# Feed-forward layer one moved to the transposes' banks, a tanh gate, expert scores from rows before their last normalisation, and self attention 8 groups behind cross attention

## The reference

```
x = LN(x + attention_1head(x))                        # W1..W4, 112x112 scores
t = crossattn(x, context, 16 heads of 16, mask);  t = LN(t @ co + x) * g + b
t = selfattn(t, 16 heads of 16);                  t = LN(t @ so + t) * g + b
t = LN(gelu(t @ fi + fib) @ fo + t) * g + b           # 256 -> 1024 -> 256
x = LN(x + t)                                         # "x5"
scores = x @ centroids.T; expert = argmax; alpha = sigmoid(score of the chosen)
y = x + relu(LN(x)*gamma_e+beta_e @ W1_e + b1_e) @ W2_e + b2_e     # 8 experts
x = LN(alpha*y + (1-alpha)*x)
```

## Time and profile before

| what | value |
|---|---|
| median of 3 runs | 472.16 us |
| profiled execution, its own time | 475.34 us |
| its span | 473.3 us |
| TensorE busy | 414.8 us (88%) |
| VectorE, ScalarE, GpSimd busy | 270.6, 243.3, 127.8 us |
| granted TensorE clock, mean | 0.939 |

### The profile page before, as it was taken

How to read it: one execution, slowest core, us unless ns; L and a number is a source line. 1 busy time by engine, 2 the same in 40 slices (tenths; PEclk the granted TensorE clock), 3 DMA queues, 4 the chain that set the end, 5 groups by cost and what they waited for, 6 DMA issues and landing times.

```text
span 473.3 us, 10486 instructions
## 1 busy us (share of the span) xinstructions
PE 414.8 (88%) x3672; PEld 347.0 (73%) x3672; DVE 270.6 (57%) x936; ACT 243.3 (51%) x822; POOL 127.8 (27%) x256
## 2 busy tenths in 40 slices
PE   6888999999999999999979797967988358998991
PEld 6766778878787887878768686756878247997991
DVE  4486766685666876867655255357255651443522
ACT  0305785785689878887887735520433002322320
POOL 4271202131032221212222132234043306231323
PEclk9999999999999999999989987985998669999997
DMA  8994100101010060000000980004802012111001
GB/s 224 304 383 100 38 10 16 35 15 35 2 48 2 2 225 2 16 1 3 1 2 2 366 345 1 1 11 176 377 10 90 29 56 81 35 34 35 25 24 35
DMA packets 10341, 37.87 MB, mean 80 GB/s; under 512 B 1440, under 2 KB 5776, under 8 KB 8400
## 3 DMA queue, kind: packets, MB, share of 16 engines
q1 hardware_dynamic: 8064, 28.40, 17.4%
q10 hardware_dynamic: 976, 5.60, 3.4%
q0 software_dynamic: 1248, 3.18, 2.1%
HBM read 32.13 MB, written 5.04 MB: 79 GB/s over the span
## 4 chain that ended last, share of the span: by engine, by line
PE 52%; DVE 6%; ACT 5%; issue 5%; DMA 2%; POOL 1%; DVEq 0%; POOLq 0%; ACTq 0%; SPq 0%
PE bank_scores L674 8%; PE bank_pt L572 7%; PE bank_out L689 7%; PE bank_scores L610 6%; PE bank_out L619 5%; PE bank_out L460 4%; PE bank_scores L556 3%; PE bank_out L446 3%; PE bank_out L594 2%; ACT arena L1080 2%; PE bank_scores L562 2%; PE bank_out L453 2%; ACT arena L1069 1%; DVE stats L747 1%; ACT arena L1089 1%
## 5 line engine op out<-in xcount | busy, mean ns | idle before, releaser
L1089 ACT ACTIVATE arena<-bank_pt 125x448 f32<-125x448 f32 (+1 forms) x128 | 67.4, 546 | 71.3 <-PE bank_pt L572 66.2
L572 PE MATMUL bank_pt<-ident,arena 112*125 112x112 f32 (+1 forms) x512 | 75.3, 280 | 4.5 <-ACT arena L1095 2.6
L870 DVE CUSTOM_DVE_ANT_0 arena<-bank_scores,arena 112x375 f32<-112x375 f32 x128 | 64.6, 544 | 25.3 <-PE bank_scores L562 18.0
L1069 ACT ACTIVATE arena<-arena,negmaxc 112x375 f32<-112x375 f32 x128 | 76.9, 604 | 2.6 <-DVE negmaxc L870 2.4
L572 PEld LDWEIGHTS bank_pt<-ident,arena 112*125 112x125 f32 (+1 forms) x512 | 63.2, 177 | 16.5 <-ACT arena L1089 6.4
L460 PE MATMUL bank_out<-arena 128*112 128x256 f32 (+1 forms) x224 | 59.3, 392 | 2.5 <-DVE arena L836 0.9
L1169 POOL TENSOR_TENSOR vareps<-meanvar,scal 112x1 f32<-112x1 f32 (+1 forms) x50 | 9.7, 194 | 173.6 <-DVE meanvar L750 128.5
L1124 ACT ACTIVATE arena<-bank_scores,consts 128x128 f32<-128x128 f32 x80 | 22.9, 370 | 60.0 <-PE bank_scores L674 46.0
L446 PE MATMUL bank_out<-arena 128*128 128x112 f32 x320 | 42.7, 288 | 5.2 <-POOL scal L1140 4.4
L460 PEld LDWEIGHTS bank_out<-arena 128*112 128x112 f32 (+1 forms) x224 | 37.9, 186 | 11.6 <-issue 3.3
L446 PEld LDWEIGHTS bank_out<-arena 128*128 128x128 f32 x320 | 41.0, 201 | 6.9 <-POOL scal L1140 4.3
(11 more groups left out here) (153 smaller groups left out, 634.2 us busy)
## 6 DMA issues: line engine op xcount, KB each, us to landing
arena<-moe SPq DMA_DIRECT2D x8, 2048.0 KB, 13.5
arena<-ctxT SPq DMA_DIRECT2D x8, 375.0 KB, 5.9
arena<-weights ACTq DMA_DIRECT2D x2, 1024.0 KB, 18.6
arena<-mask SPq DMA_DIRECT2D x8, 164.1 KB, 3.5
x_slots<-arena SPq DMA_DIRECT2D x8, 130.0 KB, 25.0
arena<-x_slots SPq DMA_DIRECT2D x8, 130.0 KB
arena<-fi ACTq DMA_DIRECT2D x1, 1024.0 KB, 24.0
arena<-fo ACTq DMA_DIRECT2D x1, 1024.0 KB, 27.2
```

The lines of the kernel that those rows point to most:

```text
L572: last = nc.tensor.transpose(dst[0:kp, j * S:(j + 1) * S], probs[0:S, (n % 2) * HG + j, c * kp:(c + 1) * kp], ident[0:S, 0:S])
L870: v.tensor_tensor_reduce(out=probsC[0:S, i % (2 * HG)], in0=score_bank[j][0:S, 0:KX], in1=masks[0:S, u % 2], scale=-1.0, scalar=3.0e38, op ...
L1069: a.activation(probsC[0:S, i % (2 * HG)], probsC[0:S, i % (2 * HG)], ACT.Exp, bias=negmax["c"][0:S, u, at:at + 1], scale=-1.0, accum_out=s ...
L1089: a.activation(probsT[0:kp, n % RT, c], pt_bank[PT[stage, i] % RP][0:kp, 0:HG * S], ACT.Copy).then_inc(pt_free, 1)
```

## The change

Five things, in one new order of the list:

- f1 writes to the two transposes' banks, in pieces that fill 448 columns of one bank: 2 chunks for two batches, 4 chunks for one, 16 pieces in all. Each piece is an entry of its own in the list, with its own due number. qk no longer waits for f1, and f2 waits piece by piece.
- The gate is 0.25 + 0.25 * tanh(best / 2). VectorE makes best * rstd * 0.5, ScalarE the Tanh, VectorE one step more.
- The transposes zx read the row before its last normalisation (behind zf, not zb). The scores with the centroids are then corrected: gap = src - mean * sum(centroid), and the largest gap is chosen; the division by the deviation enters only in the gate. The sums of the centroids come from two more matmuls in aw.
- LAG is 8, so there are 40 rounds, the last 8 with self attention alone.
- The tables of due numbers are others, with a further table SHIFT of some 240 single steps.

```diff
-ROUNDS = FC // RS
+PIECES = [FC * len(batches) * S // 448 for batches, _ in FEED]
+FIRST_PIECE = [sum(PIECES[:q]) for q in range(len(FEED) + 1)]
...
-LAG = 10
+LAG = 8
...
-FEED_STAGES = {"f1": 0.35, "f2": 1.69, "zf": 2.6, "zb": 3.72, "zn": 4.52, "zx": 4.62, "sc": 5.75, "rk": 6.77}
+FEED_STAGES = {"f1": -0.71, "f2": 0.66, "zf": 1.61, "zb": 3.44, "zn": 3.66, "zx": 3.44, "sc": 4.76, "rk": 5.85}
+PIECE_PACE = (0.14,)
+SHIFT = {("zx", 0): -0.04, ("aqk", 0): -0.01, ("aw", 0): -0.13, ("at", 0): -0.17, ("av", 0): -0.01, ("ab", 0): -0.09,
...
-PT, _ = number({"as": 1, "at": 1, "ct": 1, "st": 1, "pr": 1})
+PT, _ = number({"as": 1, "at": 1, "ct": 1, "st": 1, "pr": 1, "f1": 1})
...
-SCORED, _ = number({"qk": 1, "f1": RS})
+SCORED, _ = number({"qk": 1})
...
+                    pe.wait_ge(setup, 10)
+                    dst = out_slot(slot + C + 1)
+                    for k in range(C):
+                        last = mm(dst[0:S, 0:E], ones[:, 0:S], consts[:, COLS["cent"] + k * E:COLS["cent"] + (k + 1) * E],
+                                  start=k == 0, stop=k == C - 1)
+                    last.then_inc(out_full, 1)
...
-                    opened = {"a": "ay", "c": "cy", "s": "sy", "z": "zf"}[kind]
-                    pe.wait_ge(norm_done, FINISHED[FINISHES[opened], i] + 1)
-                    transposed_rows(slot, x1[0:S, i] if kind in "az" else ybuf[0:S, OPENED[opened, i] % NR])
+                    opened, finished = {"a": ("ay", "ab"), "c": ("cy", "cb"), "s": ("sy", "sb"), "z": ("zf", "zf")}[kind]
+                    pe.wait_ge(norm_done, FINISHED[finished, i] + 1)
+                    transposed_rows(slot, x1[0:S, i] if kind == "a" else ybuf[0:S, OPENED[opened, i] % NR])
...
-                    for b in range(RS):
-                        f = h * RS + b
-                        score_slots((stage, i), b)
+                    dst = pt_slot(PT[stage, i])
+                    for at, f in enumerate(chunks_of):
                         for k in range(C):
-                            last = mm(score_bank[b][:, 0:n], fi_sb[:, k, f * 128:(f + 1) * 128], x3T[:, k, batches[0] * S:batches[0] * S + n],
-                                      start=k == 0, stop=k == C - 1)
-                        last.then_inc(score_full, 1)
+                            last = mm(dst[:, at * n:(at + 1) * n], fi_sb[:, k, f * 128:(f + 1) * 128],
+                                      x3T[:, k, batches[0] * S:batches[0] * S + n], start=k == 0, stop=k == C - 1)
+                    last.then_inc(pt_full, 1)
...
-                    pe.wait_ge(hidden_ready, FC * (q + 1))
                     dst = out_slot(slot)
-                    for f in range(FC):
-                        last = mm(dst[0:S, 0:D], hiddenT[:, q % 2, f, j * S:(j + 1) * S], fo_sb[:, f], start=f == 0, stop=f == FC - 1)
+                    for p in range(FIRST_PIECE[q], FIRST_PIECE[q + 1]):
+                        pe.wait_ge(hidden_ready, HIDDEN["f1", p] + 1)
+                        for f in pieces(p)[3]:
+                            last = mm(dst[0:S, 0:D], hiddenT[:, q % 2, f, j * S:(j + 1) * S], fo_sb[:, f], start=f == 0, stop=f == FC - 1)
...
-                    v.tensor_reduce(best[0:S, i:i + 1], src[0:S, 0:E], AX.X, ALU.max).then_inc(best_ready, 1)
-                    dve.wait_ge(best_ready, i + 1)
-                    v.scalar_tensor_tensor(marked[0:S], src[0:S, 0:E], best[0:S, i:i + 1], rev[0:S], ALU.is_equal, ALU.mult)\
+                    dve.wait_ge(stats_ready, k + 1)
+                    v.scalar_tensor_tensor(gap[0:S], minus_centroids[0:S], meanvar[0:S, k % NR, 0:1], src[0:S, 0:E], ALU.mult, ALU.add)\
                         .then_inc(out_free, 1)
                     dve.wait_ge(out_free, slot + 1)
+                    v.tensor_reduce(best[0:S, i:i + 1], gap[0:S], AX.X, ALU.max).then_inc(best_ready, 1)
+                    dve.wait_ge(best_ready, i + 1)
+                    link(v.scalar_tensor_tensor(marked[0:S], gap[0:S], best[0:S, i:i + 1], rev[0:S], ALU.is_equal, ALU.mult))
+                    linked()
...
+                    dve.wait_ge(rstd_ready, k + 1)
+                    v.tensor_scalar(best[0:S, i:i + 1], best[0:S, i:i + 1], rstd[0:S, k % NR], 0.5, ALU.mult, ALU.mult).then_inc(best_scaled, 1)
...
-                    link(v.tensor_scalar(ex[0:S, i:i + 1], ex[0:S, i:i + 1], 1.0, 2.0, ALU.add, ALU.mult))
-                    linked()
-                    v.reciprocal(xrows[0:S, i, ALPHA:ALPHA + 1], ex[0:S, i:i + 1]).then_inc(alphaed, 1)
+                    v.tensor_scalar(xrows[0:S, i, ALPHA:ALPHA + 1], ex[0:S, i:i + 1], 0.25, 0.25, ALU.mult, ALU.add).then_inc(alphaed, 1)
...
-                    act.wait_ge(best_ready, i + 1)
-                    a.activation(ex[0:S, i:i + 1], best[0:S, i:i + 1], ACT.Exp, scale=-1.0).then_inc(exped, 1)
+                    act.wait_ge(best_scaled, i + 1)
+                    a.activation(ex[0:S, i:i + 1], best[0:S, i:i + 1], ACT.Tanh).then_inc(exped, 1)
```

More of the change, by code:

```diff
@@ L331, in pt_read, with scores_read, pieces @@
             stage = stage_of_pt[n]
+            if stage[0] == "f1":
+                return hidden_ready, HIDDEN[stage] + 1
             return (probs_ready, PROBS[stage] + 1) if stage[0] == "as" else (pt_free, COPIED[stage] + 1)
-        rounds = [stage for stage in STEPS if stage[0] in ("qk", "f1")]
-        def scores_read(stage, b):
-            kind, n = stage
-            if kind == "f1":
-                return [(hidden_ready, HIDDEN[stage] + b + 1)]
+        def scores_read(n, b):
             return [(scores_masked, n * HG + b + 1)] * (n < GROUPS) + [(probs_ready, PROBS["sm", n - LAG] + b + 1) for _ in range(n >= LAG)]
+        def pieces(i):
+            q = next(q for q in range(len(FEED)) if i < FIRST_PIECE[q + 1])
+            batches, per = FEED[q][0], FC // PIECES[q]
+            return q, batches, len(batches) * S, range((i - FIRST_PIECE[q]) * per, (i - FIRST_PIECE[q] + 1) * per)
         def all_probs(kind, n):
@@ L428, in out_slot @@
                 return out_bank[n % RO]
-            def score_slots(stage, banks):
-                k = rounds.index(stage)
-                for read in scores_read(rounds[k - 1], banks) if k else ():
-                    pe.wait_ge(*read)
             def pt_slot(n):
@@ L548, in _ @@
                 elif stage == "qk":
-                    score_slots((stage, i), HG - 1)
+                    for read in scores_read(i - 1, HG - 1) if i else ():
+                        pe.wait_ge(*read)
                     if i < GROUPS:
@@ L598, in _ @@
                 elif stage == "f1":
[L599 to L601 removed]
+                    q, batches, n, chunks_of = pieces(i)
+                    if i == FIRST_PIECE[q]:
                         if q == 0:
```

73 lines of the change are left out of this document (37 added, 36 removed), and 39 rows, old and new, of the table SHIFT.

## The result

The changed kernel takes 444.32 us (median of 4 runs, 442.99 to 445.75), before 472.67 us (4 runs on the same chip, 472.06 to 473.27). The ratio is 0.9413, 95% interval 0.9391 to 0.9435: 5.9% faster. Of the named cases rival B (the clock stays full, 448.8) is the nearest.

What follows compares the result with a forecast made beforehand. TensorE bounds it: dense in cross attention, then 18.7 us idle at clock 0.88 from 220 to 360 us. Terms -8.5 - 7.0 - 0.9 + 1.0 + 0.5 = -14.9 us give 457.3 us from 472.16; range 448 to 468.

Steps and rivals of the forecast that it cites:

- rival B: Whole kernel: the clock stays full, giving all 13 us, and idle time gives 11: 448.8 us; chance 0.14.
- idle of TensorE, 220 us to the last f2: After cross attention runs out: 18.7 us idle falls to 10.2, so 8.5 us less; ends 14.0 and 0.
- the clock: 220 to 360 us: low granted clock costs 13 us, between bounds 6.1 and 16.8; 7 us saved, ends 0 and 13.
- behind the last f2: Tail after the last feed-forward product: un-normalised score rows and shorter gate save 0.9 us; ends +0.5 and -2.1.
- rounds (lag 8): Self attention 8 groups behind: projection nearer to first scores, waits up to 2.4 us over eight batches; taken as +1.0.
- start: Kernel start: two batches, not three, projected before the first scores, so the keys' bias is waited for; +0.5 us, 0 to +2.0.
- the half: Clock term: half of the 13 us kept back, since several 0.9 us waits close together might let the clock fall.
- the walk: New order followed from the last cross scores on: waits of 4.7 us in sum, the longest 0.9 us.
- rings and queues that a walk doesn't see: Idle term after the last cross scores: 5.5 us added for unseen waits, about a third of what before has.
- piece 6: Layer one's piece 6, counted from 0: waits about 0.9 us, the copy ahead queued behind an exponential with a table load.
- Table loads: ScalarE: nine loads of 1283 ns instead of eight, none for the gate; each adds its whole length to its link.

Runs made afterwards that it cites:

- e4: Changed kernel with the scores of self pair 38 moved ahead of the transposes zx 1, adding one TensorE wait: 452.38 us, ratio 0.9519 to the kernel before.
- e6: Changed kernel with the transposes for the expert scores taken from normalised rows again: 455.77 us, ratio 0.9672 to the kernel before.
- e9: Kernel before with f2 of batch 0 moved ahead of the scores of self pair 36, into the 1.91 us gap: ratio 0.9998.
- e7: Changed kernel with the gates of batches 3, 4 and 5 earlier in the order: ratio 0.9405 to the kernel before.
- e11: Changed kernel with only the gate of batch 3 moved ahead of the rank step of batch 4: 444.82 us, ratio 0.9405 to the kernel before.
- e3: Kernel before with lag 8 and the changed kernel's cross, self and pair offsets, feed-forward part as it was: ratio 1.0543.
- e10: Changed kernel with the expert gate computed by Exp again instead of Tanh: 447.74 us, ratio 0.9473 to the kernel before.
- e5: Kernel before with f2 of batch 0 moved ahead of the scores of self pair 37, one pair late for the gap: ratio 1.0005.
- e1: Changed code (banks and pieces, tanh, un-normalised rows) run in the order and lag 10 of the kernel before: 476.75 us, ratio 1.0024.
- e2: Changed kernel with layer one's sixteen pieces in blocks per batch again, not spread: 459.76 us, ratio 0.9731 to the kernel before.
- e12: Changed kernel itself run once more, on the chip of the run with one gate moved: 444.63 us, ratio 0.9407 to the kernel before.
- e8: Changed kernel with the gates of batches 3 to 5 earlier and the rank steps of batch 6 later: ratio 0.9392 to the kernel before.

## Why the forecast was wrong

The sign, the place and the mechanism of the two large terms were right; the size was half of what came. Step by step, by the windows above:

| step | forecast, us | measured, us |
|---|---|---|
| idle of TensorE, 220 us to the last f2 | -8.5 | -13.2 |
| the clock | -7.0 | -15.1 |
| behind the last f2 | -0.9 | -0.1 |
| rounds (lag 8) | +1.0 | -0.5 |
| start | +0.5 | -0.6 (idle, 0 to 60 us) |
| experts | 0 | -1.7 |
| span in all | -14.9 | -31.2 |

*The step that failed is the clock term: "I take half, 7 us saved".* Its two factors were both low. The first was what there was to win, taken as 13; it was 15.1. Had I multiplied the low time by TensorE's busy share and not guessed between the bounds, it would have come out: 2 x 0.12 x 146.65 x (127.83 / 146.65) / 2 = 15.3 up to the last f2, and 14.6 for the prediction's own window up to 360 us. It is an estimate: it takes TensorE to be as busy in the low time as in the rest. The second was the half, kept back because the walk left waits of 0.7 to 0.9 us close together. The longest that came is 0.58, and from 220 us to the last f2 the clock is 1.00. e4, e6 and e9 show the other side: behind gaps of 1.79 to 4.02 us the same matmuls took up to 1.85 times as long. The doubt about gaps close together had something in it, though: in the first 40 us of the changed kernel waits of 0.91 and 0.68 us follow each other, and the clock fell behind them in one execution and not in the other (last section). What decides there, no run here was made to show. By the Trainium skill (TensorE: Matmul & The Clock Gate, HAM oscillation) half of the throttled time is lost: that would be 17.6 us here. The trace has 15.1, and TensorE was idle for an eighth of the stretch.

*The second step is the 5.5 us for "rings and queues that a walk doesn't see".* The walk's own 4.7 us was close to the 5.6 that are there, though its single waits were not: the third piece waited 0.49, not 0.7, piece 6 (at 283.10) no more than 0.13 and not 0.9, and the other waits were smaller and more. So the sum of the walk was right in part by luck. The added 5.5 us had no row under it. Both errors come from not trusting the walk: it left 14.0 us less idle and no wait above 1 us, and with the whole 13 of the clock that gives 472.2 - 14.0 - 13 + 0.6 = 445.8 us. Rival B, with 11 for the idle time, gave 448.8.

*The tail* had only VectorE's queue in its sum (the rank steps, which do stand in the way), and left out GpSimd's: three scatters of about 1 us stand ahead of the variance (rows above). The transpose's wait fell by 1.0 us, but the copy, forecast 0.9 us earlier, came 0.2 later. Where fewer scatters are in the way the edit shows about what was forecast: e7 and e11 take 19.3 and 19.6 us from the last f2's start to the experts, e6, whose variance was taken up at once, 20.2. Its larger worth is elsewhere, which e6 shows and the forecast did not name: zx no longer stops TensorE at the earlier batches.

*Lag and start* were given costs (1.0 and 0.5 us) and had none that shows. e3 can't price the lag. *Table loads* came out as read from the order; e10 shows that a load more costs about 0.3 us on average, not 1.28, where ScalarE has room.

*The experts'* 1.7 us don't belong to the change. In the fourteen profiles this part takes from 86.9 to 91.7 us with the same code; e5 and e9, in the order of before, have 86.9 and 87.7. And the two profiles that are compared lie on opposite sides: before's execution took 475.34 us against a median of 472.67, the changed kernel's 443.95 against 444.32. So of the 31.2 us of span about 28 are the change, which is what the medians give.

There is no gain without the order (e1), and in the order the spread of the pieces (e2), the un-normalised rows (e6) and the tanh (e10) are worth 12.3, 10.5 and 2.2 us of the stretch. These don't add up to a whole, since each was measured with the rest in place. That the move to the transposes' banks is needed for the order is argued and not shown: layer one spread in the score banks wasn't tried.

## What to carry to other kernels

When TensorE's granted clock is below 1.00 in a stretch, price the loss as low time times busy share, halved (15.3 us here, 15.1 measured). Then ask of the planned order how long its longest wait is, beside the waits of your own traces: here waits of up to 0.58 us left the clock full for 94 us, behind waits of 1.8 us and more it fell, and with waits of 0.7 to 1.2 us close together it did either (last section). If all that is left is as short as the first kind, book the whole loss as won. Small edits that take a dependency out of TensorE's way (a transpose that need not wait for a normalisation) are worth more for the order that they allow than for the chain that they shorten, so test them in the new order, not in the old. Before filling a gap by hand, look whether the filler hangs, by a bank or a queue, on the engine that made the gap: in e9 it did, and nothing was saved.

## What the runs showed of the hardware

The start differs between executions of the same program. In TensorE's timeline the first records and a projection at 30 us, first in the first profile of the changed kernel, then in the second (e12):

```profile
4.50 5.80 PE L488 MATMUL bank_out<-arena 128*128 128x112 f32 x32 [4.50 <-DMA arena<-weights]
...
28.07 0.66 PE L561 MATMUL bank_out<-arena 112*112 112x256 f32 x2 [0.90 <-DVE arena L833]
...
29.59 2.33 PE L488 MATMUL bank_out<-arena 128*128 128x112 f32 x16 [0.68 <-DVE arena L868]
```

```profile
4.42 6.97 PE L488 MATMUL bank_out<-arena 128*128 128x112 f32 x32 [4.42 <-DMA arena<-weights]
...
29.16 0.66 PE L561 MATMUL bank_out<-arena 112*112 112x256 f32 x2 [0.91 <-DVE arena L833]
...
30.68 3.26 PE L488 MATMUL bank_out<-arena 128*128 128x112 f32 x16 [0.68 <-DVE arena L868]
```

The first 32 records take 1.17 us more in the second; why stays open, since the granted clock from 4 to 6 us is 1.00 in both. Then 16 records behind the same two waits take 3.26 us there, against 2.33 in the first; the granted clock from 30 to 40 us is 0.83 in the second and 1.00 in the first. e8 is like the second (3.23 us, 0.83), e7 and e11 like the first (2.33, 1.00). The old order has such a place too, ahead of its last cross scores: waits of 0.75, 1.22 and 0.70 us within 7 us. Behind them these scores take 1.43 us in the profile of before and 1.61 in e5, at granted clocks of 0.77 and 0.68 from 238 to 244 us, but 0.90 us in e1 and e9, at 1.00. So the same waits don't always bring the same clock.

The last cross scores come at 242.73 and 244.83 us in these two. A change of 1 us can't be seen in medians of five runs over that; it shows in a stretch that starts behind it.

A Tanh behind a Gelu needed no table load (none at L1162 in the changed kernel); with Exp in its place (e10) there were four loads at the gate and three more at the Gelus. An indirect scatter holds GpSimd's queue for about 1.0 us (eight at L1270, 0.96 to 1.22 us).
